# Graph layer, mixer and expert layer in one kernel: the per-step add to the accumulator comes two steps later instead of one

## What is computed

```
Wh = xn @ W                                     # 4 heads of 64
e  = leaky_relu(Wh[src]·a_src + Wh[dst]·a_dst)  # the reference shifts e by its maximum
h_new[row] = sum over its edges of exp(e) * Wh[edge_col] / sum over its edges of exp(e)
x = x + relu(layernorm(h_new + Wh) @ ffn_w + ffn_b) + mixer(xn)
x = x + experts(layernorm(x))
```

## Time and profile before

| | us |
|---|---|
| median of 2 runs | 3582.39 |
| profiled execution, its own time | 3581.44 |
| its span | 3579.6 |
| VectorE busy | 2671.9 (75%) |
| TensorE busy | 2741.9 (77%) |
| GpSimd busy | 2249.7 (63%) |
| ScalarE busy | 1700.0 (47%) |

### The profile page before, as it was taken

One profiled execution on the slowest core, in us unless ns is written; L12 is line 12 of the kernel. 1 busy time (PEld: TensorE's weight loads), 2 busy tenths in 40 slices (PEclk: granted clock), 3 DMA queues, 4 the chain that ended last, 5 costly groups with the idle time before them and its releaser, 6 DMA issues. The chain is left out here.

```text
span 3579.6 us, 68996 instructions
## 1 busy us (share of the span) xinstructions
PE 2741.9 (77%) x13448; PEld 1697.1 (47%) x13448; DVE 2671.9 (75%) x5718; ACT 1700.0 (47%) x5062; POOL 2249.7 (63%) x2442
## 2 busy tenths in 40 slices
PE   3888826777777777787888888887886548888994
PEld 1444414444444444434444444444454336776994
DVE  8999998989989899877768777777785755545132
ACT  3888725444444444333334333333343125655773
POOL 5877757777777777766767766666776332224043
PEclk8998868999999999999999999999998779998997
DMA  1322226556555555899999999999976444344263
GB/s 54 100 97 96 89 69 163 152 152 153 152 146 155 153 150 152 191 230 230 235 225 234 228 230 226 229 237 213 232 193 169 128 142 132 121 147 149 84 191 118
DMA packets 402402, 585.83 MB, mean 164 GB/s; under 512 B 69100, under 2 KB 269738, under 8 KB 401892
## 3 DMA queue, kind: packets, MB, share of 16 engines
q1 hardware_dynamic: 293736, 326.05, 36.3%
q0 software_dynamic: 85552, 236.37, 25.5%
q10 hardware_dynamic: 22860, 20.83, 2.1%
HBM read 498.16 MB, written 84.82 MB: 163 GB/s over the span
## 5 line engine op out<-in xcount | busy, mean ns | idle before, releaser
L957 POOL DMA_INDIRECT room<-table,room x1564 | 1566.1, 1001 | 612.8 <-issue 389.8
L2171 PE MATMUL bank<-room 128*128 128x260 f32 x3520 | 921.1, 407 | 354.0 <-DVE room L1654 179.0
L2171 PEld LDWEIGHTS bank<-room 128*128 128x128 f32 x3520 | 658.6, 197 | 606.8 <-issue 518.9
L1654 DVE TENSOR_TENSOR room<-room,bank 128x1024 f32<-128x1024 f32 x440 | 532.8, 1211 | 62.7 <-issue 31.0
L1195 ACT ACTIVATE bank<-room 128x16 f32<-128x16 f32 x440 | 81.3, 185 | 832.0 <-DVE room L1648 812.6
L2210 PE MATMUL bank<-room,kvm 128*33 128x512 f32 (+1 forms) x832 | 397.5, 602 | 21.0 <-DVE room L1699 21.0
L1699 DVE TENSOR_TENSOR room<-room 128x1024 f32<-128x1024 f32 (+1 forms) x208 | 242.1, 1164 | 149.2 <-DMA room<-qt_dram 149.1
L1188 ACT ACTIVATE spare<-away,ones 128x512 bf16<-128x512 bf16 x440 | 317.6, 722 | 52.1
L1987 DVE TENSOR_TENSOR planes<-bank,spare 128x256 f32<-128x256 f32 x119 | 50.5, 424 | 351.2 <-PE bank L2368 304.9
L1185 ACT ACTIVATE away<-spare,minus_p 128x512 bf16<-128x512 bf16 x440 | 310.7, 706 | 1.5 <-DMA spare<-rows_dram 1.0
L1618 DVE TENSOR_TENSOR room<-bank,row_step 128x512 f32<-128x512 f32 x440 | 300.2, 683 | 0.2 <-DVE bank L1608 0.2
(11 more groups left out here) (326 smaller groups left out, 4294.4 us busy)
## 6 DMA issues: line engine op xcount, KB each, us to landing
room<-qt_dram SPq DMA_DIRECT2D x384, 256.0 KB
spare<-rows_dram SPq DMA_DIRECT2D x440, 128.0 KB
room<-qt_dram SPq DMA_DIRECT2D x512, 64.0 KB
room<-table,room POOLq DMA_INDIRECT x1564
kv_dram<-room SPq DMA_DIRECT2D x49, 324.0 KB, 2.2
room<-kv_dram SPq DMA_DIRECT2D x196, 81.0 KB
y_dram<-planes SPq DMA_DIRECT2D x119, 128.0 KB, 1.8
room<-xs_dram ACTq DMA_DIRECT2D x110, 128.0 KB, 2.2
```

The lines of the kernel that those rows point to most:

```text
L957: pool.indirect_dma_start(G[:, k.slot, u, :], None, table, bass.IndirectOffsetOnAxis(ap=ixbuf[:, k.slot, u:u + 1].bitcast(I32), axis=0)).t ...
L1654: dve.tensor_tensor(Gw[:, h, :, 0:C].rearrange("p u (h d) -> p u h d", h=GH), G[:, bass.ds(slot, 1), :, 0:C].rearrange("p a u (h d) -> p ( ...
L2171: ins = pe.matmul(pbank[1 + h][:, 0:TW], OH[:, s, u, :], Gw[:, h, u, :], start=(u == 0), stop=(u == U - 1))
```

## The change

`add` for step k - 1 was called in step k; now `add` for step k - 2 is. The word's tile number is taken for two steps back, the first step with an add is step 2, and behind the loop two adds are left where there was one. No wait was edited: `sum_rows(k)` still waits for the add of step k - 2.

```
         dve.wait_ge(s_pTc, 5)
         o.then(dve.tensor_copy(words[:, 0:PLAN - 1], gneed[:, 1:PLAN]))
-        o.then(dve.scalar_tensor_tensor(words[:, 1:PLAN - 1], istep[:, 0:PLAN - 2], float(PLAN), words[:, 1:PLAN - 1], ALU.mult, ALU.add))
+        o.then(dve.scalar_tensor_tensor(words[:, 2:PLAN - 1], istep[:, 0:PLAN - 3], float(PLAN), words[:, 2:PLAN - 1], ALU.mult, ALU.add))
...
-                if k.after(1):
-                    add(k + -1, tile)
+                if k.after(2):
+                    add(k + -2, tile)
                 if (k + 3).inside(STEPS):
                     one_hot(k + 3)
...
         for i in range(LAPS_Q, LAPS):
             lap(i, q_extra(NQG, i - LAPS_Q))
+        add(At(LAPS - 1, 2, 4), ahead(At(LAPS, 0, 4))[2])
         add(At(LAPS - 1, 3, 4), AGT - 1)
```

## The result

The changed kernel takes **3626.86 us** (median of 2 runs, 3619.34 and 3634.37) against 3582.39: a ratio of **1.0124**, 95% interval 1.0096 to 1.0151. That is 44.5 us slower where 21.6 was forecast. The direction was right and the time lies in the range, but the size is off by a factor of two. The profiled execution is the slower of the two, 3634.37 us with a span of 3632.6, 53.0 us longer than the span before. The runs of one kernel mostly spread by 10 to 20 us in what follows (by 32 at the most), so a ratio with its interval is what counts; single traces show where time lies.

A forecast was written before the change was run, and what follows sets the result against it. VectorE and GpSimd were taken to bound the unit part, the DMA engines the query part. Terms 5 + 4 + 4 + 1.3 + 3.4 + 1.3 + 2.5 = 21.5 us over 3581.4 gave 3603, as median 3604 us; range 3578 to 3655.

The forecast's parts named there:

- No gain from the relaxed wait: Adds in the steps: relaxing their wait gives 0, at best 29.5 us, since `one_hot` behind waits for the same count.
- Sums released by the add: Every step: `sum_rows` starts when VectorE's add ends, not when `weigh` ends, 2.3 us later in a normal step.
- (a): Ends of the four head pairs: `kv_turn`, behind the last sums, comes later; 5 us lost, bounds 0 and 9.1.
- (f): Register instruction in one step of four, 110 times: 2.5 us lost, bounds 0 and 11.
- (b): Query part: late s2 transpose delays `weigh(s0)` 1.93 us per lap, mostly hidden by data waits; 8 us, at most 85.
- the rival on the clock: Query part: s0 sums run at TensorE's lower clock after longer idle time; 80 us uncovered, 3684 us, or 0 covered; chance 0.04.
- (c): Last `y_part` of the last query lap: its sums begin later, delaying expert weights and stores; 1.3 us, bounds 0 and 1.3.
- (d): Laps after the last query lap: same s2 delay without features, 1.7 us in two laps; 3.4 us, bounds 0 and 3.4.
- (e): End of the steps: the sums of step 438 begin after the add; 1.3 us, bounds 0.9 and 3.
- the last query group: Its 4 laps have small loads and no data waits: 7.7 us of s2 delay, some 3.5 absorbed by gather waits; 4 us.
- Nothing moves: Rival: GpSimd and DMA engines set both parts, so the time stays at 3580 to 3586 us; chance 0.2.
- The s2 chain without any cover: Rival, query part: `weigh(s0)` stalls 1.93 us in 44 laps and data waits do not shrink; 85 us, 3681 us; chance 0.09.

## Why the prediction was right in kind and wrong in size

**No gain from the relaxed wait**: right. Idle time before the adds went from 29.5 to 32.3 us; without "issue" it stayed, 16.5 and 16.4, so none of it passed to `one_hot`, whose 4.5 us for the sums are new.

**Sums released by the add**: right, 478.8 us of waits on L1662 where `weigh` had been the releaser.

**(a), (f), unit part**, forecast 7.5: measured 8.3 in the pair of traces, and 1.0028 or 10 us with the change in this part alone. The sum fits better than its terms: at the first pair VectorE's wait for `kv_turn` did not grow (3.57 us before, 2.96 after), and no run shows (f) by itself. At the third pair 3.3 us of lateness were forecast and VectorE's wait rose from 0.79 to 5.05 us, +4.3:

```profile
1254.86 3.57 PE L2172 MATMUL bank<-room 128*128 128x260 f32 x8 [3.71 <-DVE agg L1662]
...
1260.37 0.29 DVE L1777 TENSOR_SCALAR kvm<-bank,room 128x66 f32<-128x66 f32 x1 [5.05 <-PE bank L2191]
```

The surplus has its row in the same trace: the last sums of the lap took 3.57 us in place of 1.99, behind 3.71 us in which TensorE had stood idle.

**(b), the s2 chain**: the stall was right, the cover was not. Forecast were 2.2 us at `weigh` in about 44 laps, 100 us in all, and it is 101.0 us in 44; data waits were to fall to about 70, and they fell to 67.5. Added waits are 77.4 + 48.0 = 125.4 us, of which data waits took back 81.6: 43.8 us remain over the part and the last laps, where (b) had 8. Two steps failed, and with them two costs went missing. The first is (b)'s "the stall is taken out of that wait, and nothing is lost". It took the time at which the data land as given. But SyncE's loads stand behind a wait for the late ScalarE, and so 1.8 us of each stall's cover is pushed back with it. Undoing this alone is worth 19 us with both chains (1.0129 to 1.0077) and 22 with the s2 chain alone (1.0094 to 1.0033). The second is "covered by the same data waits, 0, which is in my sum", in the rival on the clock. The s0 chain adds 48.0 us at `normalise_y`, and costs 16 us with the loads on time (1.0077 against 1.0033). The forecast left it out of the last ten laps as well, where there are no such data waits to cover it; by the traces 7 to 12 us of its cost stand there. Loads 19, s0 chain 16 and the unit part's 10 us make 45, the whole loss. Each is a difference of ratios whose intervals reach 0.001 to 0.002 either way, so it is known to within some 4 to 8 us, and taken in another order the parts come out otherwise (the s0 chain at 13 us with late loads, 20 with the s2 chain gone).

**(c), (d), (e), and the last query group** (4 of (b)), together 10: measured 16.0 in this pair of traces, and 13.1 in the other trace of the changed kernel. The last query group's four laps alone have +10.3 in place of 4, and what is behind them +5.7 in place of 6. The 4 for the s2 chain was about right: with the s0 transposes ahead the group has +4.9. The rest is the s0 chain, which none of these terms names, so the agreement of (c) to (e) is luck: with the s0 transposes ahead they are 1.1 us, and 1.6 with both.

**The rivals.** "Nothing moves" is out. The s2 chain without any cover (3681 us) is out: two thirds of what the chains add was covered. It was to decide when the DMA share falls by over 2%; the share fell by 1% only, while the rate fell by 3% (229 to 222 GB/s): the share did not show what the rate did. The clock rival had the s0 chain's mechanism, longer sums behind the data wait and a waiting `normalise_y`, priced at 80 us or 0. It is 48.0 us of waits. And the forecast's upper end is not what its terms give: 3604 + 14.2 + 25.7 is 3644 us, not 3650.

TensorE's sums mostly took 2.0 us, but 3.04 behind 2.87 us of idle time, 3.57 behind 3.71, and 3.81 behind 4.00; the clock of the part fell from 0.95 to 0.90. What the Trainium skill's page "TensorE: Matmul & The Clock Gate", section "Why this matters for your kernels", asks, to keep idle gaps between bursts of matmuls short, agrees with these rows. But the gap right ahead does not tell the level by itself: other s0 sums of the trace took as long behind less than 1 us:

```profile
2336.33 3.53 PE L2172 MATMUL bank<-room 128*128 128x260 f32 x8 [0.85 <-DVE agg L1662]
```

The time did not follow the clock by itself: with both transposes ahead it is 0.90 too, at a loss of 0.2%.

## What to carry to other kernels

When a producer's buffers stay two, moving the consumer later moves the producer's start later: list every reader behind it in its queue in one lap, not the worst one, and ask in which laps nothing covers it. And before a stall is written off as hidden under a wait for data, follow it to the queue that issues the loads: if anything there waits in order for the stalled engine, the data come later too, and a reordering of that queue is the cheap repair.

## What the runs showed of the hardware

The DMA share stayed at 1.01 to 1.02 while the rate moved between 222 and 230 GB/s with when the loads were issued (222 with a gap of 1.83 us, 226 with the same kernel's loads moved ahead): a share near one did not mean that the queues had no time to lose. And six products of zeros ahead of the s0 sums, 1.46 us of TensorE work, lifted the granted clock of the query part from 0.90 to 0.95, and 16 to 0.98.
